# A graph layer on one core: blocks from the highest node down, gathers without a loop, and two engines that take a round's edges and its unit in turns

## What is computed

```python
dst = jnp.minimum((100000 * uniform(key, (50000,)) ** 2.0).astype(int32), 99999)
_o = jnp.argsort(dst, stable=True); src = src[_o]; dst = dst[_o]
...
msg = jnp.concatenate([x[src], edge_attr], axis=1) @ W1 + b1          # 96 -> 128
agg = jax.ops.segment_sum(msg, dst, num_segments=100000)
out = x + jnp.concatenate([x, agg], axis=1) @ W2 + b2                 # 192 -> 64
return (out - mean(out)) / sqrt(var(out) + 1e-5)
```

## Time and profile before

| | |
|---|---|
| median of 3 runs | 802.4 us (802.13 to 803.19) |
| span of the profiled execution | 801.0 us |
| busy: TensorE, weight loads | 615.5 us, 544.4 us |
| busy: VectorE, GpSimd, ScalarE | 522.7 us, 423.9 us, 398.6 us |
| mean granted clock of TensorE | 0.843 of full speed |
| gathers | 392, mean 1004 ns |

### The profile page before, as it was taken

The page is one execution under the profiler, slowest core; times in us unless marked ns, Lnnn a source line. Parts: engine busy times, 40 slices in busy tenths (PEclk is TensorE's granted clock), DMA queues, the critical chain, the costliest instruction groups (busy, mean ns, idle before and its releaser), DMA issues. The chain is left out here.

```text
span 801.0 us, 29016 instructions
## 1 busy us (share of the span) xinstructions
PE 615.5 (77%) x8418; PEld 544.4 (68%) x8419; DVE 522.7 (65%) x1826; ACT 398.6 (50%) x2012; POOL 423.9 (53%) x514
## 2 busy tenths in 40 slices
PE   1345445677778888888898898989898888878785
PEld 1344435566767777777777787878777777768675
DVE  3670111354465648858887788788787787878876
ACT  0011122102234344444567777777777777757655
POOL 5676766711676766475467777767466445200000
PEclk9655555657688779979999999999999999989988
DMA  2121222200223233333345545555455455533432
GB/s 63 28 37 36 37 37 34 57 9 12 61 54 82 59 86 79 79 78 79 100 110 139 127 122 139 129 136 147 115 139 144 110 132 134 134 86 115 126 97 81
DMA packets 168753, 71.47 MB, mean 89 GB/s; under 512 B 61570, under 2 KB 162447, under 8 KB 168720
## 3 DMA queue, kind: packets, MB, share of 16 engines
q1 hardware_dynamic: 104592, 51.74, 22.7%
q0 software_dynamic: 12544, 12.87, 8.5%
q10 hardware_dynamic: 51584, 6.41, 5.1%
HBM read 45.37 MB, written 25.60 MB: 89 GB/s over the span
## 5 line engine op out<-in xcount | busy, mean ns | idle before, releaser
L363 POOL DMA_INDIRECT feat<-in_x,src_now x392 | 393.6, 1004 | 255.4 <-issue 94.6
L775 DVE TENSOR_SCALAR onehot<-node_of_col,group_base,dst_of 128x256 bf16<-128x256 bf16 x952 | 287.4, 348 | 106.1 <-issue 78.9
L473 PEld LDWEIGHTS ps_y<-z_window,onehot 128*128 128x128 bf16 x5712 | 202.6, 101 | 65.8 <-DVE z_window L778 46.0
L473 PE MATMUL ps_y<-z_window,onehot 128*128 128x64 bf16 x5712 | 226.7, 198 | 26.6 <-DVE z_window L778 23.5
L574 ACT ACTIVATE square<-ps_y 128x64 bf16<-128x64 f32 x784 | 162.7, 239 | 135.8 <-PE ps_y L464 133.2
L574 ACT ACTIVATION_READ_ACCUMULATOR square<-ps_y 128x1 f32 x784 | 159.5, 224 | 0.0
L539 ACT ACTIVATE feat_t<-ps_t 97x512 f32<-97x512 f32 x98 | 58.6, 598 | 179.8 <-PE ps_z L400 159.9
L400 PE MATMUL ps_z<-wz,feat_t 97*128 97x64 f32 x784 | 123.1, 324 | 24.6 <-DVE z_rest L700 24.5
L400 PEld LDWEIGHTS ps_z<-wz,feat_t 97*128 97x128 f32 x784 | 118.0, 238 | 33.2 <-DVE z_rest L700 31.8
L392 PE MATMUL ps_t<-ident,feat 128*97 128x128 f32 x392 | 72.3, 333 | 86.8 <-DMA feat<-in_x,src_now 63.7
L464 PE MATMUL ps_y<-wx,x_t 128*128 128x128 f32 x784 | 118.4, 296 | 13.1 <-issue 8.7
(11 more groups left out here) (107 smaller groups left out, 226.2 us busy)
## 6 DMA issues: line engine op xcount, KB each, us to landing
xin<-in_x SPq DMA_DIRECT2D x97, 256.0 KB
out<-yout SPq DMA_DIRECT2D x97, 256.0 KB
feat<-in_x,src_now POOLq DMA_INDIRECT x392
feat<-in_edge_attr ACTq DMA_DIRECT2D x97, 64.0 KB
z<-in_src SPq DMA_DIRECT2D x1, 192.0 KB
z<-in_dst SPq DMA_DIRECT2D x1, 192.0 KB
xin<-in_x SPq DMA_DIRECT2D x1, 128.0 KB
out<-yout SPq DMA_DIRECT2D x1, 128.0 KB
```

Source lines behind the costliest of these rows:

```text
L363: nc.gpsimd.indirect_dma_start(out=feat[h][:, half * CB + c, 0:C], out_offset=None, in_=x[:, :], in_offset=bass.IndirectOffsetOnAxis(ap=sr ...
L473: mm = nc.tensor.matmul(ps_y[h][:, col:col + C], onehot[h][:, g, s, a, :], z_window[h][:, g, s, part * C:(part + 1) * C], start=False, sto ...
L775: ins = nc.vector.tensor_scalar(onehot[h][:, g, s, :, :], node_of_col[:, :, :], base, dst_of[:, bass.ds(firsts[g] + (at + s), 1)], ALU.add ...
```

## The change

Five things are done together.

1. Blocks and chunks run from high node numbers down: block b of the program is block 97 - b of the nodes (`x_block`, `out_block`, `group_base`, `block_base`), the columns of `src_idx`, `dst_of` and of the two bound rows are copied in reverse, the edge features of a batch stand in reverse slots (`feat_slot`). The cut last block is now the first one; its `xin` is cleared by GpSimd and its loads stand first in SyncE's queue.
2. The table of open units gets a cap: not over `AHEAD` = 2.125 blocks per round.
3. GpSimd's gathers are written out, 98 times four without a loop; the index columns are read from `src_idx` itself, so the copy to `src_now` and its waits go.
4. TensorE's and ScalarE's first unit of a round is mixed with the round's edge work in smaller pieces (`unit_in_round`, `full_round`); more units of the round follow as before, and a round without one takes the old order. TensorE's loop is unrolled by two rounds, so the branch on parity goes. VectorE's order is not changed.
5. SyncE's `free_yout` waits for one store more on `h` = 0, and its loop steps with a register `top`. Two semaphores (`x_go`, `s_idle`) are raised and not waited for.

```diff
@@ GpSimd
-            def gather(k, h, half):
+            def gather(k, h):
                 wait_rounds(pool, gathered[h], k, 16 * CB)
-                nc.gpsimd.tensor_copy(src_now[h][:, :], src_idx[:, bass.ds(2 * CB * k + CB * h, CB)]).then_inc(s_now, 1)
-                pool.wait_ge(s_now, 2 * k + h + 1)
-                if not (isinstance(k, int) and k < 2):
+                if k >= 2:
                     pool.wait_ge(feat_used[h], k - 1)
-                pool.sem_inc(s_go)
                 for c in range(CB):
+                    col = (2 * k + h) * CB + c
                     nc.gpsimd.indirect_dma_start(
-                        out=feat[h][:, half * CB + c, 0:C], out_offset=None, in_=x[:, :],
-                        in_offset=bass.IndirectOffsetOnAxis(ap=src_now[h][:, c:c + 1], axis=0)).then_inc(gathered[h], 16)
-            for k in range(3):
-                for h in range(2):
-                    gather(k, h, k % 2)
-            with pool.Fori(3, PAIRS - 1, 2) as k:
...
+                        out=feat[h][:, feat_at(k) + feat_slot(c), 0:C], out_offset=None, in_=x[:, :],
+                        in_offset=bass.IndirectOffsetOnAxis(ap=src_idx[:, col:col + 1], axis=0)).then_inc(gathered[h], 16)
+            for k in range(PAIRS):
+                for h in range(2):
+                    gather(k, h)
@@ GpSimd, constants
-            nc.gpsimd.iota(group_base[:, :], pattern=[[GN, BLOCKS * G]], base=0, channel_multiplier=0,
+            nc.gpsimd.iota(group_base[:, :], pattern=[[-BN, BLOCKS], [GN, G]], base=(BLOCKS - 1) * BN, channel_multiplier=0,
@@ TensorE
+            def unit_in_round(k, half, u):
+                turn(k, 0, half)
+                message(k - 1, 0)
+                second, third = load_counts(u, 0)
+                open_sum(u, 0)
+                first_sum(u, 0, 0)
+                turn_x(u, 0)
+                first_sum(u, 0, 1)
+                turn(k, 1, half)
+                first_sum(u, 0, 2)
+                first_sum(u, 0, 3)
+                rest_sums(u, 0, second, third)
+                message(k - 1, 1)
+                second, third = load_counts(u, 1)
+                open_sum(u, 1).then_inc(hots_used[0], 1)
+                first_sum(u, 1, 0)
+                turn_x(u, 1)
+                first_sum(u, 1, 1)
+                first_sum(u, 1, 2)
+                dense(u, 0, None)
+                first_sum(u, 1, 3)
+                rest_sums(u, 1, second, third)
+                dense(u, 1, hots_used[1])
+            def full_round(k, half):
+                done, now = read_units(mybir.EngineType.PE, k - LAG)
+                with pe.If(now > done):
+                    unit_in_round(k, half, nc.s_assert_within(done, 0, PAIRS - 1, skip_runtime_bounds_check_because="so the table is made"))
+                    more = pe.snap(done + 1)
+                    with pe.If(now > more):
+                        with pe.Fori(more, now) as u:
+                            unit(u)
...
+                with pe.Else():
+                    edge_round(k, half)
...
-            with pe.Fori(LAG + 2, PAIRS - 1) as k:
-                edge_round(k)
-                for_units(pe, mybir.EngineType.PE, k - LAG, unit)
-            edge_round(PAIRS - 1, loads=2)
+            with pe.Fori(LAG + 2, PAIRS - 1, 2) as k:
+                full_round(k, 0)
+                full_round(k + 1, 1)
+            edge_round(PAIRS - 1)
@@ ScalarE
+                with act.If(now > done):
+                    for h in range(2):
+                        keep_feat(k, h)
+                        load_ea(k + 1, h)
...
+                    z_highs(k - 1)
+                    for h in range(2):
+                        keep_x(u, h)
+                    z_mids(k - 2)
+                    for h in range(2):
+                        keep_y(u, h)
+                    root(u)
...
+                    act.sem_inc(s_idle)
@@ VectorE, the table
+            link(nc.vector.scalar_tensor_tensor(out=open_block[:, :], in0=round_no[:, :], scalar=AHEAD,
+                                                in1=open_block[:, :], op0=ALU.mult, op1=ALU.min))
             link(nc.vector.tensor_copy(units[:, :], open_block[:, :]))
             link(nc.vector.tensor_scalar(units[:, :], units[:, :], 1, None, ALU.arith_shift_right))
@@ SyncE
             def load_x(k, h, src_ap):
                 wait_rounds(sp, x_used[h], k)
+                sp.sem_inc(x_go)
                 sp.dma_start(xin[h][:, :, :], src_ap).then_inc(x_loaded[h], 16)
             def free_yout(k, h):
-                wait_rounds(sp, out_stored[h], k, 16)
+                if not (isinstance(k, int) and k == 0):
+                    sp.wait_ge(out_stored[h], 16 * k + (16 if h == 0 else 0))
                 sp.sem_inc(yout_free[h])
...
+            with sp.Fori(2, PAIRS - 1) as k:
+                top = sp.snap(BLOCKS - 2 * k)
+                for h in range(2):
+                    load_x(k + 1, h, x_full[top - (3 + h)])
+                store_round(k - 1, top + 1)
```

More of the change, by code:

```diff
@@ L43 @@
 LAG = 2
+AHEAD = 2.125
 FAR = float(1 << 20)
@@ L188, in gnn_residual_layernorm @@
         squared = sem2("squared")
+        s_idle = sem("act_after_units")
         s_root = sem("std_ready")
@@ L402, in message, with edge_round @@
                 mm.then_inc(z_done[h], 1)
-            def edge_round(k, loads=1):
-                if isinstance(k, int):
-                    turn(k, 0)
-                    turn(k, 1, loads)
-                else:
-                    for half in range(2):
-                        with pe.If(k % 2 > 0 if half else k % 2 < 1):
-                            for h in range(2):
-                                turn(k, h, half=half)
+            def edge_round(k, half=None):
+                for h in range(2):
+                    turn(k, h, half)
                 for h in range(2):
@@ new lines, in open_sum, with pair_sum @@
+                return nc.tensor.matmul(ps_y[h][:, :], ones_bf[:, :], b2rows[:, :, :].rearrange("p n c -> p (n c)"),
+                                        start=True, stop=False)
+            def pair_sum(h, g):
+                for s in range(2):
+                    for a in range(A):
+                        col = (g * A + a) * C
+                        for part in range(3):
+                            mm = nc.tensor.matmul(ps_y[h][:, col:col + C], onehot[h][:, g, s, a, :],
+                                                  z_window[h][:, g, s, part * C:(part + 1) * C], start=False, stop=False)
+                return mm
@@ L481, in block_sum, with first_sum, rest_sums @@
+            def first_sum(k, h, g):
+                b = 2 * k + h
+                pe.wait_ge(window_ready, G * b + g + 1)
+                pe.wait_ge(hot_ready, G * b + g + 1)
+                pair_sum(h, g).then_inc(group_summed, 1)
+            def rest_sums(k, h, second, third):
+                b = 2 * k + h
                 with pe.If(second > 0):
@@ L506, in block_sum, with dense @@
                                         mm.then_inc(hotx_used[s], 1)
+            def dense(k, h, hots):
                 pe.wait_ge(x_ready[h], k + 2)
-                dense(0).then_inc(hots_used[h], 1)
-                for g in range(1, G - 1):
-                    dense(g)
-                dense(G - 1).then_inc(y_done[h], 1)
+                for g in range(G):
+                    mm = nc.tensor.matmul(ps_y[h][:, g * A * C:(g + 1) * A * C], x_t[h][:, g * P:(g + 1) * P],
+                                          wx[:, :], start=False, stop=(g == G - 1))
+                    if g == 0 and hots is not None:
+                        mm.then_inc(hots, 1)
+                mm.then_inc(y_done[h], 1)
             def unit(u):
@@ L516, in unit @@
                 for h in range(2):
-                    block_sum(u, h)
+                    second, third = load_counts(u, h)
+                    open_sum(u, h)
+                    for g in range(G):
+                        first_sum(u, h, g)
+                    rest_sums(u, h, second, third)
+                    dense(u, h, hots_used[h])
+            def unit_in_round(k, half, u):
[29 more added lines that the diff above has]
+                            unit(u)
+                    nc.tensor.reg_mov(pairs_done, pairs_done)
+                with pe.Else():
+                    edge_round(k, half)
             for h in range(2):
@@ L593, in unit, with full_round @@
                 root(u)
+            def full_round(k):
+                done, now = read_units(mybir.EngineType.Activation, k - LAG)
+                with act.If(now > done):
+                    for h in range(2):
+                        keep_feat(k, h)
+                        load_ea(k + 1, h)
+                    u = nc.s_assert_within(done, 0, PAIRS - 1, skip_runtime_bounds_check_because="so the table is made")
+                    z_highs(k - 1)
[5 more added lines that the diff above has]
+                    root(u)
+                    more = act.snap(done + 1)
```

(7 more changed lines are left out.)

157 lines of the change are left out of this document (74 added, 83 removed).

## The result

The changed kernel took **1249.55 us** (median of 4 runs, 1243.95 to 1254.94) beside 802.8 for the kernel before: a ratio of 1.558, interval 1.553 to 1.563. The forecast of 713.5, its range to 758 and its sign were all wrong. Only rival 4 gave a time above 900, and it was a rival about the clock, not about what follows.

A forecast was written before the change was run, and what follows sets the result against it. Early rounds were bound by GpSimd's gathers, later ones by VectorE's queue, TensorE close behind. Along VectorE's queue the terms gave 692.1 us, plus 20 of losses a 712.1 span, plus 1.4 a median of 713.5; range 690 to 758.

The forecast's parts named there:

- rival 4: TensorE's clock stays low: all 44 rounds at 1.2 GHz, giving 915 us; chance 0.02.
- Parity branches on TensorE: Branches in TensorE's loop, gone with the index copies' waits: claimed to change nothing on VectorE's path.
- low part of loop round 4: VectorE's `z_lows` start in loop round 4, after the round 3 gathers: 65.5 us, bounds 61 and 70.
- rounds 4 to 47, second and third pairs: VectorE's 44 one-unit rounds at 10.84 (477.0), four more units (32.8), second pairs (51.9), one third-pair turn (1.5).
- 20 of losses: Added to VectorE's sum: 6 for first units at low clock, 5 for clock lapses, 9 for new hand-overs.
- chain of the last round's edges: Last edges from transposes to low part, with no unit left to cover them: 13 us, bounds 8 and 18.
- last unit: The former first unit, with 18 third-pair turns, now at the end with nothing beside it: 41.8 us.
- end: From VectorE's last one-hot to the end of the span: 8.6 us.
- Gathers written out: GpSimd's gathers take 10.7 us a round and stay hidden; the saving, some 5 us, counts at the start only.
- Rival 1: GpSimd's gathers get no denser, 12.35 us a round, round 38 is 29 late: 742 us; chance 0.13.
- rival 3: Shared port: every gather takes 1.454 us beside busy VectorE, a round 14.0, round 38 is 93 late: 807 us; chance 0.03.
- rival 2: Hand-overs over `turn_x` and SyncE replace the waits; VectorE loses 1.25 in each of 44 rounds: 768 us; chance 0.11.

The follow-up runs named there:

- h1: The changed kernel with TensorE's unrolling alone undone (106 KB loop; mixed order and inner loop stay; count held by a register maximum): 790.8 us, ratio 0.986.
- h3: The kernel before with two never-run copies of a unit in TensorE's loop (146 KB), assertions added: 1342.7 us, ratio 1.673.
- f1: The changed kernel with TensorE's and ScalarE's loops and order of before, unit counts held by one register maximum: 713.8 us, ratio 0.890.
- f2: f1 with the gathers back in a loop, with the index copy and its waits: 748.7 us, ratio 0.931.
- e4: The kernel before with three never-run copies of a unit in TensorE's loop (193 KB), assertions added: 1809.75 us, ratio 2.255.
- f3: e3 with the first half's transposes and message ahead of the table's load and test, and a register maximum (56 KB): 728.35 us, ratio 0.905.
- e3: The changed kernel's mixed order in a 58 KB loop: no unrolling, no inner loop, cap of one unit a round, assertions: 806.9 us, ratio 1.006.
- e1: The changed kernel with TensorE's and ScalarE's loops in their form of before (53 KB), unit counts asserted: 737.8 us, ratio 0.913.
- h2: The changed kernel, still unrolled, without the inner loop for further units, cap one unit a round (109 KB): 1044.4 us, ratio 1.300.
- h4: The kernel before with only the assertions on the loaded unit counts added: 828.65 us, ratio 1.031.

## Why the prediction was wrong, and where it was right

**The step that failed** is half a sentence in the part on what is moved: "*Parity branches on TensorE* and the index copies' waits go: nothing on VectorE's path." The unrolling was read as branches taken away. Together with the second copy of the unit in each round it quadrupled TensorE's loop, 53 to 204 KB by my count, and this had no term, no bound and no rival. What the runs showed in its place: the loop was fetched anew in every turn, 13.5 packets in 47.8 us (378 us of "issue" in the run), and with the unrolling alone undone 16 packets and 790.8 us remain (h1). The chances were spread over mechanisms of the data path alone, and 0.95 for faster rested on that list being whole. The row that would have asked the question was on the page: `q8 instruction: 23, 0.38, 0.2%`. 0.38 MB is about seven times a loop of 53 KB, so a loop of 45 rounds cannot be fetched anew each turn; from there the question follows what happens as it grows to 204. The rows of before could not have shown the limit, but they allowed a rival.

The Trainium skill, page Runtime: NRT & Kernel Launch, section "Instruction fetch mechanics", says that an engine's instruction memory is small (128 KiB for TensorE), refilled in 16 KiB blocks over a queue of its own, and that a taken branch out of the window forces a fetch. The packets of 16 KB are what the trace shows. A loop of 106 KB by my count stayed and one of 109 was fetched again, below that figure, as far as the count can be trusted. The jumps do not follow that rule in every case: h3's rounds without a unit jump over the unit and two copies of it, some 47 KB each, and load nothing. The page also holds that the fetch is mostly hidden; here a packet took 1.3 us, and TensorE stood 1.5 to 2.2 us for each. The measurement decides.

**The rest of the sum**, read in f1, which has all of the change except the unrolled loop and the mixed order:

| term of the span | forecast | f1 |
|---|---|---|
| low part of loop round 4 | 65.5 | 65.9 |
| rounds 4 to 47, second and third pairs | 563.2 and 20 of losses | 636.23 - 65.87 = 570.4 |
| chain of the last round's edges | 13 (8 to 18) | 656.05 - 636.23 = 19.8 |
| last unit | 41.8 | 701.88 - 656.05 = 45.8 |
| end | 8.6 | 712.0 - 701.88 = 10.1 |
| together | 712.1 | 712.0 |

That the sums agree is luck in part. The losses come to 7 and not 20: the slices of the clock are at 9 tenths or more from the sixth to the 36th of f1, all but one, and 9 of the 20 were for hand-overs of the mixed order, which f1 does not have. There are also 472 window copies and not 476. The chain was mis-sized and outside its bound: two waits for ScalarE's parts, 7.05 and 4.54, stand in it, since nothing is queued to fill them. The last unit and the end were each a little dearer. The errors are -12.8, +6.8, +4.0, +1.5 and +0.4.

**Point by point.** *Start and rounds of one unit*: right; 10.90 us against 10.84, the start within 0.4. *Gathers written out*: the mechanism was right, "their saving counts at the start only" is not: f2 shows 35 us, of which 3.7 are at the start (its low part in round 4 begins at 69.6, f1's at 65.9). Rival 1's arithmetic, 29 us late at round 38, fits what happens without the writing out. *Last gather near 605*: 599.7. *Port*: GpSimd's gathers in f1 have a mean of 1014 ns beside a VectorE at 73%, near the 1042 of the earlier trace rows; rival 3 is refuted. *Clock low throughout*: 915 was its most, so it can't make 1249.6. The clock of 0.72 in the changed kernel goes with a TensorE that is busy half the time, and no run shows which brings the other about: in e4's turns without a unit the clock was 1.00 with TensorE busy for 5.3 of 27.3 us. *Hand-overs (rival 2)*: 0.2 a round holds where the table's test is covered (11.12 in f3 against 10.90). As the change writes it, the test is not covered, and a round costs 2.3 more (13.44 in e3 against 11.13 in e1), nearly double the 1.25 of the rival; the prediction did not see the test's move at all. So even if loading cost nothing, the change as written would, as far as h1 stands for it, lie near 790.8, above the range, with 77 us of the gain given back.

## What to carry to other kernels

Count the instructions in an engine's loop before unrolling it or writing a body in twice, and read the instruction queue's row of the page. In these kernels TensorE's loops up to some 106 KB by count were loaded once; those of 109 KB and more were loaded again and again, TensorE lost 1.5 to 2.2 us for each 16 KB, and code that never runs could be part of it. When a circle of engines wait for each other, look for the one whose idle time ends at "issue" once in a turn, and check that no queue between engines (here SyncE's) hides another engine behind such a wait. Put queued matmuls ahead of a register load and a branch on it.

## What the runs showed of the hardware

- **TensorE's loops of up to 106.0 KB by my count were loaded once, larger ones again and again.** 106.0 KB (h1): 16 packets in the whole run; 108.8 KB, unrolled (h2): 209, and 9 packets a turn, more than the loop's length; 146 KB (h3): 270.
- **Instructions jumped over can be loaded too**: e4 fetched 10 to 11 packets a turn, some 180 KB, while its three copies, some 140 KB by count, never ran. But h3's rounds without a unit, with two copies, loaded nothing.
- **A packet of 16 KB took 1.3 us itself** (changed kernel, 2.0% of 16 x 1242.1 us over 298), and TensorE stood 1.5 to 2.2 us for each (table; e4's turns without a unit).
- **Assertions on two loaded counts, on three engines, cost 27 us in 45 rounds** (h4), 0.6 us each round, on a path where I had expected 3 to 10 in all; one register maximum on each engine in their place leaves f1 at the forecast's time.
- **An uncovered register load with its branch held TensorE 2.2 us** a round (e3).
